# Row stage of a two-layer graph kernel as one scan over two partitions, an unread TensorE product in each step of layer 1, and register loads in ones and twos on SyncE and GpSimd

## The reference

```python
# layer 0, per edge and head (H = 8, HD = 32), n nodes
score = einsum('ehd,ehd->eh', K[src], Q[dst]) / sqrt(HD) + edge_bias
m     = segment_max(score, dst);  ex = exp(score - m[dst])
attn  = ex / segment_sum(ex, dst)[dst]
out   = segment_sum(attn[:, :, None] * V[src], dst)   # then Wp, layer norm, a feed-forward net
# layer 1, per edge and head
e     = leaky_relu(el[src] + er[dst], 0.2)            # el, er: 8 numbers per node
a     = softmax of e over the edges of one dst
out   = segment_sum(feat[src] * a[:, :, None], dst)
```

## Time and profile before

| what | us |
|---|---|
| median of 3 runs | 6000.13 (5995.2 to 6009.43) |
| the profiled execution | 6002.02 |
| its span, first to last instruction | 6000.1 |
| edges of layer 0, first to last gather | 369.5 to 2649.0 |
| edges of layer 1, first to last gather | 3664.8 to 5743.6 |

### The profile page before, as it was taken

The page is one execution under the profiler, slowest core; times in us unless marked ns, Lnnn a source line. Parts: engine busy times, 40 slices in busy tenths (PEclk is TensorE's granted clock), DMA queues, the critical chain, the costliest instruction groups (busy, mean ns, idle before and its releaser), DMA issues. The chain is left out here.

```text
span 6000.1 us, 128155 instructions
## 1 busy us (share of the span) xinstructions
PE 5427.5 (90%) x26094; PEld 4291.0 (72%) x26094; DVE 4908.2 (82%) x12464; ACT 3153.2 (53%) x10275; POOL 3755.0 (63%) x4022
## 2 busy tenths in 40 slices
PE   8978888888888888888999998988999999999988
PEld 5556666666666666667999996766777777777766
DVE  4469999999999999996777775777787787878864
ACT  3446666566666665643333334555555565555533
POOL 1147666766666666644444446777777777777733
PEclk9999999999999999999999997787777777777789
DMA  5679889998988888872222224777777777777767
GB/s 176 211 223 291 284 284 290 290 289 281 289 281 285 285 282 285 283 232 83 83 85 85 84 85 141 218 218 219 219 217 218 216 221 218 221 218 217 220 201 229
DMA packets 723032, 1313.66 MB, mean 219 GB/s; under 512 B 109087, under 2 KB 502131, under 8 KB 722420
## 3 DMA queue, kind: packets, MB, share of 16 engines
q0 software_dynamic: 200192, 634.41, 37.3%
q1 hardware_dynamic: 444802, 422.18, 23.6%
q10 hardware_dynamic: 77426, 250.73, 10.9%
HBM read 964.16 MB, written 342.73 MB: 218 GB/s over the span
## 5 line engine op out<-in xcount | busy, mean ns | idle before, releaser
L826 PE MATMUL bank<-ev,oh 128*128 128x264 f32 x7040 | 2275.3, 453 | 94.5 <-DVE ev L1294 93.5
L534 POOL DMA_INDIRECT Gf<-kv_tab,srcs x1564 | 1573.4, 1006 | 721.3 <-issue 511.2
L534 POOL DMA_INDIRECT Gf<-ft_tab,srcs x1564 | 1603.5, 1025 | 484.1 <-issue 412.8
L826 PEld LDWEIGHTS bank<-ev,oh 128*128 128x128 f32 x7040 | 1459.8, 220 | 348.3 <-DVE ev L1294 128.6
L826 PE MATMUL bank<-Gf 128*128 128x128 f32 (+3 forms) x6480 | 1263.6, 346 | 21.8 <-ACT Gf L815 15.4
L1294 DVE TENSOR_TENSOR ev<-Gf,ex 128x528 f32<-128x528 f32 x1760 | 1228.5, 698 | 2.0 <-ACT ex L698 1.2
L826 PE MATMUL bank<-qs,oht 128*128 128x256 f32 x3520 | 955.1, 394 | 227.1 <-DVE prod L1203 226.9
L826 PEld LDWEIGHTS bank<-Gf 128*128 128x128 f32 x6480 | 966.2, 191 | 221.5 <-issue 98.6
L630 ACT ACTIVATE absd<-lane,dlocs 128x128 f32<-128x128 f32 x3520 | 1113.0, 389 | 3.6 <-DVE bms L1176 3.6
L826 PEld LDWEIGHTS bank<-qs,oht 128*128 128x128 f32 x3520 | 598.9, 190 | 438.6 <-issue 372.1
L1309 DVE SCALAR_TENSOR_TENSOR acc<-acc,same,bank 128x264 f32<-128x264 f32 x1540 | 732.0, 475 | 22.7 <-PE bank L826 20.8
(11 more groups left out here) (160 smaller groups left out, 6086.7 us busy)
## 6 DMA issues: line engine op xcount, KB each, us to landing
sums<-acc ACTq DMA_DIRECT2D x440, 528.0 KB
qs<-q_tab SPq DMA_DIRECT2D x880, 128.0 KB
qs<-dst_tab SPq DMA_DIRECT2D x880, 128.0 KB
Gf<-sums SPq DMA_DIRECT2D x196, 132.0 KB, 2.1
kv_tab<-Gf SPq DMA_DIRECT2D x98, 260.0 KB, 2.1
Gf<-in_x SPq DMA_DIRECT2D x196, 128.0 KB, 2.1
Gf<-kv_tab,srcs POOLq DMA_INDIRECT x1564
Gf<-ft_tab,srcs POOLq DMA_INDIRECT x1564
```

The costliest lines, as they stand in the source:

```text
L534: pool.indirect_dma_start(out=rows[layer][:, m % SLOTS[layer], k, :], out_offset=None, in_=tab, in_offset=bass.IndirectOffsetOnAxis(ap=src ...
L826: return nc.tensor.matmul(o, a, r, start=first, stop=end)
```

## The change

The row stage is laid on two partitions. Partition 0 holds the forward scan, partition 1 the backward scan with its elements in reversed order, so one scan instruction of 136 elements does both. To fill the second partition reversed, `row_values` uses products with an anti-diagonal matrix `anti` beside those with the identity: four products with a 2-column weight in place of three transposes. The subtraction `ct` on DVE goes; PE forms it, spread to all 128 partitions, by two products with the constant rows `minus_first` and `plus_second`, which now stand in `columns`, ahead of the two that make the columns of `xy`. PE's own `rescale` goes. ACT's `rescale` works on 128 partitions and stands at step 4, right before `factors`, where it stood at step 2.

In layer 1 PE computes in each step, between `spread` and `agg`, one product of the identity with 256 columns of a weight into bank 0; nobody waits for it or reads it.

SP loads the value that it waits on (`spans_by`) one per step, the next one right after each `landed`; in layer 1 it also loads the span of `dst_rows` one per step. POOL loads its values two at a time.

```diff
-        wlf = sb("wlf", [1, 3, H * RW + 1])
-        U = sb("U", [1, H * RW + 1])
-        Y = sb("Y", [1, H * RW + 1])
+        anti = sb("anti", [P, P])
+        minus_first = sb("minus_first", [2, P])
+        plus_second = sb("plus_second", [2, P])
+        wv = sb("wv", [2, 2, H * RW + 1])
+        uy = sb("uy", [2, H * RW])
...
-            def spans_of(layer, b):
+            def spans_by(layer, u):
                 base = layer * (NSPAN + 1)
-                return nc.values_load_multi_w_load_instructions(
-                    ready_rows[layer][:, b * ST:(b + 1) * ST], engines=[mybir.EngineType.SP], min_val=base + 1,
-                    max_val=base + NSPAN + 1)[1]
+                return sp.value_load(ready_rows[layer][:, u:u + 1], min_val=base + 1, max_val=base + NSPAN + 1)
...
-                    dst_rows(Blk(u // ST, 1), u % ST, at[u % ST])
+                    dst_rows(Blk(u // ST, 1), u % ST, spans_by(0, u))
                 v = u - RLAG[1]
                 if v >= 0:
-                    if v % ST == 0:
-                        n = spans_of(1, v // ST)
-                    landed(n[v % ST])
+                    landed(n)
+                if -1 <= v < NS - 1:
+                    n = spans_by(1, v + 1)
...
-                            if old % ST == 0:
+                            if old % 2 == 0:
                                 free = nc.values_load_multi_w_load_instructions(
-                                    free_row[0:1, old:min(old + ST, NSPAN)], engines=[mybir.EngineType.Pool],
+                                    free_row[0:1, old:old + 2], engines=[mybir.EngineType.Pool],
...
             def rescale(B):
-                act.wait_ge(E_["row"], ROW * B.c + 3)
-                act.activation(rx[:, :], ct[:, :], ACT.Relu).then_inc(E_["rx_made"], 1)
+                act.wait_ge(E_["r_mm"], B.c + 1)
+                act.wait_ge(E_["scan_b"], 2 * B.c + 2)
+                act.activation(rx[:, :], bank[7][:, 392:392 + H], ACT.Relu).then_inc(E_["rx_made"], 1)
...
+            def unread():
+                mm(bank[0][:, 0:D], ident[:, :], w_l[:, 0, :])
...
             def row_values(B):
-                for q, v in enumerate((wa[:, 0:1], scan1[:, P - 1:P], scan2[:, 0:1])):
-                    m = tr(bank[7][0:1, q * P:(q + 1) * P], v)
+                for q, (ahead, back) in enumerate(((wa[:, 1:3], wa[:, 0:2]), (last_0, first_0))):
+                    mm(bank[7][0:2, q * P:(q + 1) * P], ahead, ident[:, :], True, False)
+                    m = mm(bank[7][0:2, q * P:(q + 1) * P], back, anti[:, :], False, True)
...
             def columns(B):
                 pe.wait_ge(E_["xy_cp"], 2 * B.c + 2)
-                nc.tensor.transpose(bank[7][:, 384:385], xy[0:1, 0, :], ident[0:1, 0:1])
-                nc.tensor.transpose(bank[7][:, 385:386], xy[0:1, 1, :], ident[0:1, 0:1]).then_inc(E_["cols_mm"], 1)
+                mm(bank[7][:, 392:392 + H], minus_first[0:2, :],
+                   uy[0:2, :].rearrange("p (h c) -> p h c", c=RW)[:, :, 0], True, False)
+                mm(bank[7][:, 392:392 + H], plus_second[0:2, :],
+                   uy[0:2, H * RW - 1::-RW], False, True).then_inc(E_["r_mm"], 1)
+                mm(bank[7][:, 384:385], xy[0:2, 0, :], ident[0:2, 0:1])
+                mm(bank[7][:, 385:386], xy[0:2, 1, :], ident[0:2, 1:2]).then_inc(E_["cols_mm"], 1)
...
-            def rescale(B):
-                pe.wait_ge(E_["r_exp"], B.c + 1)
-                mm(bank[7][:, 392:392 + H], ones[0:1, :], rexp[0:1, :]).then_inc(E_["r_mm"], 1)
...
+                        if layer == 1 and B.live:
+                            unread()
...
-                r.did(V.tensor_tensor_scan(U[0:1, 0:n], w_[:, 0:n], l_[:, 0:n], -BIG, ALU.add, ALU.max))
-                r.seq(V.tensor_tensor_scan(Y[0:1, n:0:-1], w_[:, n:0:-1], f_[:, n:0:-1], -BIG,
-                                           ALU.add, ALU.max))
-                r.did(V.tensor_tensor(ct[:, :], y_[:, :, 0], u_[:, :, 0], ALU.subtract))
+                V.tensor_tensor_scan(uy[0:2, :], wv[0:2, 0, 0:H * RW], wv[0:2, 1, 0:H * RW], -BIG,
+                                     ALU.add, ALU.max).then_inc(E_["row"], 1)
```

More of the change, by code:

```diff
@@ L200, in build @@
         ats = sb("ats", [P, P + 1])
-        wa = sb("wa", [P, 1])
+        wa = sb("wa", [P, 3])
         sred = sb("sred", [P, P])
@@ L204, in build @@
         S = sb("S", [P, P])
-        scan1 = sb("scan1", [P, P])
-        scan2 = sb("scan2", [P, P + 1])
-        wlf = sb("wlf", [1, 3, H * RW + 1])
-        U = sb("U", [1, H * RW + 1])
-        Y = sb("Y", [1, H * RW + 1])
-        ct = sb("ct", [1, H])
-        xy = sb("xy", [1, 2, P])
-        rx = sb("rx", [1, H])
-        rexp = sb("rexp", [1, H])
+        scan1_0 = sb("scan1", [P, P + 1])
+        scan1, last_0 = scan1_0[:, 0:P], scan1_0[:, P - 1:P + 1]
+        scan2_0 = sb("scan2", [P, P + 2])
+        scan2, first_0 = scan2_0[:, 1:P + 2], scan2_0[:, 0:2]
+        anti = sb("anti", [P, P])
[3 more added lines that the diff above has]
+        uy = sb("uy", [2, H * RW])
+        xy = sb("xy", [2, 2, P])
+        rx = sb("rx", [P, H])
+        rexp = sb("rexp", [P, H])
         rm = sb("rm", [P, 2, H])
@@ L293, in build @@
             oht_cp oh0_made qexp prodd redd sadd smade s_tr scan_a rows_mm rows_cp row carried xy_cp cols_mm scan_b rx_made
-            r_exp r_mm rm_made m_tr dmade ex_made ev_made agg accd resc init0 init1""".split():
+            r_exp r_mm rm_made m_tr signs dmade ex_made ev_made agg accd resc init0 init1""".split():
             E_[name] = sem(name)
@@ L453, in dst_rows @@
                 sp.dma_start(qs[:, s, :], dst_tab[bass.ds(n * SPAN, SPAN)].partition_broadcast(P)).then_inc(qld[s], 16)
-            def span_rows(b):
-                return nc.values_load_multi_w_load_instructions(
-                    ready_rows[0][:, b * ST:(b + 1) * ST], engines=[mybir.EngineType.SP], min_val=1, max_val=NSPAN + 1,
-                    skip_runtime_bounds_check_because="a step's span is one of the spans or the one after them")[1]
             sp.wait_ge(S_["rec_ld"], 16 * (LC + 1))
@@ L512, in rstd @@
                                    ALU.pow).then_inc(done, 1)
[L514 removed]
+            pool.wait_ge(cm, 10)
             with pool.Fori(0, NT) as t:
@@ L620, in step_records @@
                 copy(o[:, 512:NS, e % 2], bank[7][:, 0:NS - 512], S_["x_cp"])
+            act.activation(minus_first[0:2, :], ident[0:2, 0:1].to_broadcast([2, P]), ACT.Copy,
+                           scale=-1.0).then_inc(E_["signs"], 1)
+            copy(plus_second[0:2, :], ident[0:2, 1:2].to_broadcast([2, P]), E_["signs"])
             for c in range(LC):
@@ L658, in factors @@
             def factors(B):
-                act.wait_ge(E_["r_mm"], B.c + 1)
+                act.wait_ge(E_["r_exp"], B.c + 1)
                 act.wait_ge(E_["oh0_made"], 2 * B.c + 2)
-                act.activation(rm[:, B.par, :], bank[7][:, 392:392 + H], ACT.Identity, scale=oh0[:, B.par, 0:1],
+                act.activation(rm[:, B.par, :], rexp[:, :], ACT.Identity, scale=oh0[:, B.par, 0:1],
                                bias=oh0[:, B.par, 1:2]).then_inc(E_["rm_made"], 1)
             def carried(B):
-                copy(wlf[0:1, 1, 0:H * RW].rearrange("p (h c) -> p h c", c=RW)[:, :, 0],
-                     U[0:1, 0:H * RW].rearrange("p (h c) -> p h c", c=RW)[:, :, CH], E_["carried"])
+                copy(wv[0:1, 1, 0:H * RW].rearrange("p (h c) -> p h c", c=RW)[:, :, 0],
+                     uy[0:1, :].rearrange("p (h c) -> p h c", c=RW)[:, :, CH], E_["carried"])
             def links(B):
@@ L718, in turn @@
                             row_values(A)
-                        if s == 2 and A.live:
+                        if s == 4 and A.live:
                             rescale(A)
-                        if s == 4 and A.live:
                             factors(A)
@@ L965, in turn @@
                             maxima_turned(A)
-                        if s == 3 and A.live:
-                            rescale(A)
                         if s == 5 and B.live:
@@ L977, in edge_phase @@
                     turn(Blk(b, layer))
+            pe.wait_ge(E_["signs"], 2)
             edge_phase(0)
@@ L1075, in _ @@
             c0.did(V.memset(ats[:, P:P + 1], 0.0))
+            c0.did(V.memset(wa[:, :], 0.0))
+            c0.did(V.memset(scan1_0[:, P:P + 1], 0.0))
+            c0.did(V.memset(scan2_0[:, 0:1], 0.0))
             for kvo in kvos:
@@ L1254, in row_scans @@
             def row_scans(B):
-                r = Chain(dve, E_["row"], ROW)
-                r.start(B.c)
                 dve.wait_ge(E_["rows_cp"], B.c + 1)
-                w_, l_, f_ = [wlf[0:1, q, :] for q in range(3)]
-                n = H * RW
-                r.did(V.tensor_tensor_scan(U[0:1, 0:n], w_[:, 0:n], l_[:, 0:n], -BIG, ALU.add, ALU.max))
-                r.seq(V.tensor_tensor_scan(Y[0:1, n:0:-1], w_[:, n:0:-1], f_[:, n:0:-1], -BIG,
-                                           ALU.add, ALU.max))
```

(6 more changed lines are left out.)

40 lines of the change are left out of this document (19 added, 21 removed).

## The result

The changed kernel takes **6009.03 us** in the median of 20 runs (5997.39 to 6024.38); the kernel before, beside it, 5998.9 (20 runs). The ratio is 1.0019, with a 95% interval of 1.0012 to 1.0027. The forecast was 5964, with 5925 to 5998, so it was wrong: the change costs 0.2% where a gain of 0.6% was expected. By the signs that the prediction named, the third came true (the mean block of layer 0 stayed at 20.9 us); layer 1 moved by 6 us, and SP's waits shrank as forecast.

A forecast was written before the change was run, and what follows sets the result against it. DVE was taken to bound layer 0 and POOL's unbroken gathers layer 1. 6002.0 - 35 (row stage) - 1 (shorter drain) = 5966 us against the profiled execution, or 5964 against the median, with a range of 5925 to 5998.

The forecast's parts named there:

- the third: Sign that the prediction is wrong: layer 0 stays at 20.8 us per block instead of 20.5.
- The scan's gain of 0.52 us: DVE, layer 0: one row scan on two partitions replaces three instructions, 0.87 to 0.35 us per block if nothing waits.
- the chain to the whole scan: From row scan through ACT's xy and PE's columns to DVE's scan L1271: DVE waits 0.20 us per block.
- The gain of 0.32 us per block: Layer 0's edges on DVE: 0.52 less 0.20 of waiting, over 110 blocks 35 us, bounds 57 and 11.
- The DMA engines are at a share of 0.90 and must take 1.5% more per time; I charge nothing: Layer 0: the DMA engines' higher load from DVE's shorter block was priced at nothing.
- PE in layer 0: Added PE work of 1.17 us per block fits into 2.35 us of waiting; 0.9 us stay.
- SP's loads hidden in layer 1: Single register loads add 8.5 us per block, covered by SP's 10.3 us of waiting for POOL, 1.8 left.
- POOL's loads: POOL's register loads of two run while gathers run, as those of eight did: no cost.
- The unread product buys nothing: Layer 1: PE's clock rises to about 0.95 to 1.00, no time gained, since POOL keeps 1.33 us per gather.
- The gathers, "taken as unchanged": POOL's gathers stay at 1025 ns; their 0.08 us of excess could move time by -125 to +125 us.
- The first rival: DVE's new wait at L1271, or PE's spent slack, eats layer 0's gain: 5990, between 5988 and 6000; chance 0.13.
- The slower rivals: Layer 1: SP's loads become the bound, 6074, chance 0.09; low clock, PE can't carry the product, 6339, chance 0.04.

The follow-up runs named there:

- after_land3: Changed kernel, but in layer 0 POOL issues gathers of three further spans, not two, before waiting for a landing: 5958.42 us, ratio 0.9948 to the kernel before.
- before_land3: Kernel before, with POOL issuing gathers of three further spans instead of two in layer 0 before waiting for a landing: 5989.46 us, ratio 0.9996.
- short_scan: Kernel before, with the second row scan on DVE cut to one element from the second block on: 5996.05 us, ratio 0.9999.
- short_scan_land3: Kernel before, with the second row scan cut to one element and three further spans of gathers in layer 0: 5961.10 us, ratio 0.9937.
- row_only_b: Kernel before with the new row stage alone, register loads in eights, no unread product: 6030.62 us, ratio 1.0053.
- row_unread: Kernel before with row stage and unread product, all register loads still in eights: 6002.07 us, ratio 1.0016.
- pool_eights_b: Changed kernel with POOL's register loads of two turned back into eights: 6010.58 us, ratio 1.0020 to the kernel before.
- row_land3_b: Kernel before with the row stage alone and three further spans of gathers in layer 0, no unread product: 5987.99 us, ratio 0.9990.
- unread_only: Kernel before with the unread product in layer 1 and nothing else: 6001.19 us, ratio 1.0001.
- eights_land3: Kernel before with row stage, unread product and three further spans of gathers in layer 0, register loads in eights: 5963.04 us, ratio 0.9939.
- pool_eights: Changed kernel with POOL's loads of two turned back into eights, in a job where the kernel before took 7431.13 us: ratio 1.0600.

## Why the prediction was wrong, step by step

- **The scan's gain of 0.52 us and the chain to the whole scan: right.** Scan to add are 0.35 us as forecast. xy came 0.45 + 0.51 us behind the scan's start, as forecast (0.42 + 0.04 + 0.50), PE's columns began 1.02 us behind its start and ended at 1503.49, 1.04 us later (1.16 forecast). The whole scan starts 2.10 us behind the row scan, against 0.35 + 1.62 = 1.97 without a wait: 0.13 us of waiting for 0.20. (At 0.11 us per MATMUL the prediction's working gives 0.27 + 7 x 0.11 = 1.04 us for the columns and a wait of 0.13, where it says 0.10; this cheaper row was the right one.)
- **The gain of 0.32 us per block: right in kind, a little too small.** after_land3 measures it where nothing hides it: 20.86 to 20.44 us, 0.42 per block, and 49 us over the layer where 35 were in the sum. Against before_land3, with the same reach of the gathers, it is 2300.8 to 2258.4, 42 us.
- **"The DMA engines are at a share of 0.90 and must take 1.5% more per time; I charge nothing": this is the step that failed.** It should have asked when a row lands, not how many bytes the engines can carry. The kernel before was at two limits at once: DVE at 20.8 us per block, and POOL's landing wait at almost the same pace. after_land3, short_scan and short_scan_land3 show it: with a faster DVE and two spans of reach the mean block takes 20.85 to 20.94 us in the changed kernel, row_only_b, row_unread and short_scan, where it took 20.86 before. The 35 us were lost to it in full, and it was not among the rivals. The margin that DVE's rows had in the kernel before, between SP's signal and the product, was 6.9 us in the median of 450 to 2550 us; it fell to 1.7 us. (The 7.4 us in the expectation of before_land3 hold for 1000 to 2000 us.)
- **PE in layer 0: right.** +1.17 us per block were forecast and about 1.0 measured; busy time rose from 18.4 to 19.4 per block (1862.06/101, and 1997.48/103 in after_land3), and DVE has no row of waiting for PE there.
- **SP's loads hidden in layer 1: right.** SP's wait for POOL fell from 10.3 to 164.0/110 = 1.5 us per block; 2 were forecast. The single loads took 0.50 us on the mean there, with a rival's threshold of 0.55. Before, the rows were `L389` and `L457`; after:

```profile
L391 SPq TENSOR_LOAD <-tile_row x2640: 262/429/1697, 376.7 to 5757.6; - x189
```

  The minimum of 262 ns contradicts for one register the floor of about 600 ns that the Trainium skill gives (DMA: Bandwidth & Descriptors, Latency and other measured facts), as the 267 ns of the earlier trace rows did.
- **POOL's loads: right, nothing.** pool_eights_b.
- **"The unread product buys nothing": right without the row stage, wrong beside it.** The clock did go to 0.98. But the prediction counted the row stage's PE work in layer 1 only as 2.0 us of occupancy at full clock, and gave neither it nor the product a price in time. Without the product, at the low clock, the row stage lengthens layer 1 by 27 us (row_land3_b) to 38 us (row_only_b); the product takes most of that back (28 us between the medians, 22 by the ratios 1.0053 and 1.0016). The two terms that were put at nothing all but cancel. That the stretch came out only 6 us off the forecast (2084.8 for 2079) is luck in this part. The rule of the Trainium skill (TensorE: Matmul & The Clock Gate, Terms) would have given back 520 us; unread_only, whose clock rose by 0.21, gave 0.0%. By that measurement the rule doesn't say what a kernel gains where another engine sets the pace.
- **The gathers, "taken as unchanged": open.** The prediction saw that their excess over 950 ns would be moved by a different rhythm on DVE, and took the phases as good as random. The excess does hang on DVE (see the gathers beside `ev` above), and the phases did not stay the same.
- **The first rival** (a wait eats the gain, 5990) had the gain eaten, but named the wrong wait; the measured time lies 9 us above its bounds. The slower rivals did not occur: SP's loads keep 1.5 us of slack, the clock did not stay low.
- **The rest** of the +9 us is small and not settled by experiments: four kernels at the supply's pace need 2.93 to 2.94 us per span where the kernel before needed 2.92, and gathers in layer 1 take 1024 to 1035 ns in the seven kernels with the product, 1022 to 1026 in the four without the product, the row stage or the padding. Between the means, 1030 and 1024, that is some 9 us of layer 1.

**A better version.** after_land3, the change with `LAND = (3, 4)`, takes 5958.42 us, 0.5% less than the kernel before and 0.7% less than the changed one (ratios 0.9948 and 1.0019). eights_land3 is as good with register loads as they were.

## What to carry to other kernels

An engine that is busy for the whole stage proves that it is a bound, not that it is the only one. Before pricing a faster engine, look at its suppliers: on what does the queue of the supplier itself stand most of the time, and by how much do its goods arrive early? Then test it: a longer reach of the supplier and a cheaper instruction on the engine, each alone and both together. And an instruction added on an engine with slack must be priced in each stage at that stage's clock.

## What the runs showed of the hardware

- With two further spans under way, POOL's signal that a span of two gathers of 128 rows has landed comes 4.0 to 4.2 us behind the end of the second gather at a DMA share of 0.89 to 0.90, 3.9 us at 0.86. At 0.91, with three spans under way, the engines moved 292 GB/s.
- A gather on POOL that starts within 0.45 us behind the start of DVE's `ev` takes 1274 ns on the mean, all others 973 (layer 1 of the kernel before; 1282 and 974 in row_only_b).
- The granted clock of TensorE in layer 1 was 0.75 in the kernel before and 0.96 with two MATMULs of 436 ns more in each step and nothing else changed (unread_only; the row of its page is L826 with bank<-steps,ident, x1760, since the weight lies in the tile `steps`).
- The same programs took 5990 to 6000 us and 7330 to 7430 us in different jobs, at clocks of 0.90 and about 0.81. The row stage alone cost 0.5% at the first and 4.1% at the second; with the product and half of the register loads it was 0.2% and 6.0% (pool_eights_b, pool_eights).
